# A four-layer sequence kernel: the queries of the third layer are projected between the stages of a scan, and attention is run a group deeper

## What is computed

```python
x = x + attention0(x, cond)          # 16 heads of 16
x = x + scan1(cond, x)               # 128 time steps, four Runge-Kutta stages each: tanh(q) @ coupling.T ...
# layer 2
x1  = ln(x) * (1 + scale1) + shift1                   # scale, shift, gate: from cond, one set per batch
qkv = x1 @ qkv_w + qkv_b                              # 256 -> 3 * 16 * 128
attn = softmax(einsum('bthd,bshd->bhts', q, k) * 128 ** -0.5)
x = x + gate1 * (einsum('bhts,bshd->bthd', attn, v) @ out_w + out_b)
x = x + gate2 * (gelu(x2 @ ffn_w1 + ffn_b1) @ ffn_w2 + ffn_b2)      # x2 = ln(x) * ...
x = x + gru3(cond, x)                # 128 time steps
```

## Time and profile before

| what | value |
|---|---|
| runs (three) | 1753.77, 1754.12 (median), 1755.26 us |
| profiled execution | 1756.03 us, its span 1753.9 us |
| layer 0 | 0 to 260 us |
| scan with its pieces | 260 to 933 us |
| rest of keys and values (finish_kv) | 933 to 1002.6 us |
| attention (attend2) | 1002.6 to 1349.3 us |
| norm, feed-forward, GRU | 1349.3 to 1753.9 us |
| granted TensorE clock, mean | 0.811 of full speed |

### The profile page before, as it was taken

One profiled execution on the slowest core, in us unless ns is written; L12 is line 12 of the kernel. 1 busy time (PEld: TensorE's weight loads), 2 busy tenths in 40 slices (PEclk: granted clock), 3 DMA queues, 4 the chain that ended last, 5 costly groups with the idle time before them and its releaser, 6 DMA issues. The chain is left out here.

```text
span 1753.9 us, 47524 instructions
## 1 busy us (share of the span) xinstructions
PE 1388.7 (79%) x16650; PEld 1077.1 (61%) x16650; DVE 1277.5 (73%) x7020; ACT 807.9 (46%) x3106; POOL 298.3 (17%) x568
## 2 busy tenths in 40 slices
PE   6889874445589549955985799999998489999865
PEld 4377653334466446644664688888885377777764
DVE  4357769999899989998995366666665546676654
ACT  4547843332545255525542255555553644444322
POOL 1015521111011101111111122222120301111110
PEclk8969995555589559955996999999999799999755
DMA  3000000100022002200231573546431300000000
GB/s 128 0 1 2 2 13 38 50 2 2 2 74 110 14 2 92 104 2 2 107 118 79 192 169 97 127 107 141 103 91 48 84 2 3 3 12 6 15 15 14
DMA packets 75014, 95.12 MB, mean 54 GB/s; under 512 B 5692, under 2 KB 46232, under 8 KB 73880
## 3 DMA queue, kind: packets, MB, share of 16 engines
q1 hardware_dynamic: 74336, 89.95, 17.2%
q0 software_dynamic: 272, 2.10, 0.6%
q10 hardware_dynamic: 168, 0.04, 0.0%
HBM read 54.32 MB, written 37.75 MB: 52 GB/s over the span
## 5 line engine op out<-in xcount | busy, mean ns | idle before, releaser
L933 PE MATMUL bank<-s_tanh_hi,coup_hi 128*128 128x16 f16 x2048 | 138.4, 177 | 212.7 <-ACT s_tanh_hi L923 212.4
L933 PEld LDWEIGHTS bank<-s_tanh_hi,coup_hi 128*128 128x128 f16 x2048 | 93.6, 104 | 296.8 <-ACT s_tanh_hi L923 291.1
L1408 ACT ACTIVATE prob<-bank,neg_max 128x128 f32<-128x128 f32 x256 | 90.4, 365 | 129.1 <-DVE neg_max L1457 129.1
L923 ACT ACTIVATE s_tanh_hi<-s_s 128x32 f16<-128x32 f32 x256 | 58.6, 229 | 183.5 <-DVE s_s L778 180.8
L861 POOL TENSOR_SCALAR s_p_scaled<-s_p 128x32 f32<-128x32 f32 x128 | 37.4, 293 | 602.5 <-DVE s_p L844 581.4
L933 PE MATMUL bank<-s_tanh_lo,coup_hi 128*128 128x16 f16 x2048 | 137.3, 177 | 1.8 <-DVE s_tanh_lo L772 0.2
L933 PE MATMUL bank<-s_tanh_hi,coup_lo 128*128 128x16 f16 x2048 | 128.2, 172 | 0.0
L933 PEld LDWEIGHTS bank<-s_tanh_lo,coup_hi 128*128 128x128 f16 x2048 | 90.8, 103 | 32.0 <-DVE s_tanh_lo L772 0.5
L1510 POOL TENSOR_TENSOR prob<-prob,inv 128x512 f32<-128x512 f32 x64 | 66.6, 1040 | 254.4 <-DVE inv L1476 254.4
L1724 PE MATMUL bank<-h_hi,w_h_hi 128*128 128x16 f16 x1536 | 91.2, 172 | 21.8 <-DVE h_hi L1942 21.8
L567 ACT ACTIVATE prob<-bank,neg_max 128x128 f32<-128x128 f32 x256 | 89.9, 377 | 35.6 <-DVE neg_max L515 35.6
(11 more groups left out here) (309 smaller groups left out, 4645.3 us busy)
## 6 DMA issues: line engine op xcount, KB each, us to landing
keys<-tile_stage SPq DMA_DIRECT2D x64, 256.0 KB, 2.0
values<-tile_stage SPq DMA_DIRECT2D x64, 256.0 KB, 2.4
k<-keys SPq DMA_DIRECT2D x64, 256.0 KB, 4.2
v<-values SPq DMA_DIRECT2D x64, 256.0 KB, 6.0
x<-in_L_cond_qkv_w_dram SPq DMA_DIRECT2D x2, 2048.0 KB, 7.3
x_tok<-in_x_dram SPq DMA_DIRECT2D x4, 512.0 KB, 5.5
w_stage<-in_L_cond_qkv_w_dram SPq DMA_DIRECT2D x4, 512.0 KB, 8.1
ow_stage<-in_L_cond_out_w_dram SPq DMA_DIRECT2D x4, 512.0 KB, 5.2
```

The costliest lines, as they stand in the source:

```text
L923: A.activation(th_hi[:, :], s, ACT.Tanh, scale=scale).then_inc(hi_ready, 1)
L933: ins = nc.tensor.matmul(coupled[:, B * m:B * m + B], w[:, o:o + P], th[:, B * c:B * c + B], start=(first and c == 0 and m == 0), stop=(la ...
L1408: last = A.activation(prob[:, grp % 2, h, :], bank[2 + grp % 2][:, T * h:T * h + T], ACT.Exp, bias=neg_max[:, grp % 2, h:h + 1], accum_out ...
```

## The change

Tiles become 48 to a block (`TILES`): of every 12, four are queries, four keys, four values. A plan (`plan`) places pieces by stage; the scan takes 135 tiles (48, 48 and 39), the rest of the kernel 57 (9 left over and the 48 of block 3). The high and low parts of x have one buffer in place of four, so block n's high part waits for the tiles of block n-1. The weights of queries too are split in the scan (96 pieces in place of 64), loaded in six 1 MB parts. In the scan, c = 1 is modulated on POOL (four instructions at each of four time steps), c = 0 on ScalarE (two in a stage). Centring starts at r = 10, tiles at r = 48. Keys and queries are stored so that a unit reads each as one 1 MB transfer of 8 KB rows; a tile is then stored in rows of 512 bytes. The value bias is left out of the values and goes through the output weights into the output bias (32 small products at the end of finish_kv). Attention has no projection, no value bias and no query weights; units are loaded three deep; POOL puts the queries in order of time (`turn`), one head after each group's product with the reciprocal; scores have three banks, outputs two, probabilities four buffers; an output projection of 12 matmuls is spread over two slots.

```diff
-KV_EARLY = 3
-RING = 5
-W_AT, SCALED_AT, LOW_AT, TILES_AT = (20, 72), 24, 36, 45
+EARLY = 3
+RING = 6
+TILES = 3 * H2
+W_AT = 20
...
+def plan():
+    pe, act, dve = {}, {}, {}
+    ready = lambda n: 4 * TB * (n + 1)
+    for n in range(EARLY):
+        r = ready(n)
+        for k in range(4):
+            pe[r + 2 + 2 * k] = ("mean", n, k)
+            pe[r + 20 + k] = ("var", n, k)
+            for c in range(C):
+                dve[r + 2 * k + c] = ("sum", n, k, c)
+                dve[r + 10 + 4 * c + k] = ("centre", n, k, c)
+                dve[r + 27 + 2 * k + c] = ("scaled", n, k, c)
+                dve[r + 39 + 4 * c + k] = ("low", n, k, c)
...
+        i = ready(n) + 48
+        for half in range(2 * TILES):
+            while i in pe:
+                i += 1
+            if i >= 4 * T - 1 or (half % 2 == 0 and i >= 4 * T - 2):
+                break
+            pe[i] = ("tile", n, half // 2, half % 2)
...
+                (37, ("high", n, 0)), (40, ("high", n, 1))]:
...
@@ scan1, gpsimd, behind p_scaled and g3 of step j
+                n, k = divmod(j - TB - 7, TB)
+                if n >= 0 and k < 4:
+                    pool.wait_ge(xhat_ready, 8 * n + C * k + 2)
+                    for b in range(4 * k, 4 * k + 4):
+                        last = G.tensor_scalar(xc[:, 1, TB * b:TB * b + TB], xc[:, 1, TB * b:TB * b + TB],
+                                               g.ada[:, C + 1, b:b + 1], g.ada[:, 1, b:b + 1], MUL, ADD)
+                    last.then_inc(modp_ready, 1)
@@ scan1, scalar
+            def x_high(n, c):
+                if c == 0:
+                    act.wait_ge(mod_ready, 8 * n + 8)
+                    if n:
+                        act.wait_ge(tile_full, TILES * n)
+                else:
+                    act.wait_ge(modp_ready, 4 * n + 4)
+                A.activation(g.x_hi[:, c, :], xc[:, c, :], ACT.Copy).then_inc(xh_ready, 1)
@@ finish_kv, tensor: 3 left-over tiles before the variance, 6 behind it, then block 3
+            for v in range(min(3, LEFT)):
+                tile(v)
...
+            for v in range(3, LEFT):
+                tile(v)
             pe.wait_ge(xl_ready, 2 * C)
+            for v in range(LEFT, len(todo)):
+                tile(v)
+            pe.wait_ge(g.d_ow, 16)
+            for c in range(C):
+                for h in range(H2):
+                    last = M.matmul(bank[0][:, c:c + 1], g.ow_raw[:, h, P * c:P * c + P], g.vec[:, V_VB + h:V_VB + h + 1],
+                                    start=(h == 0), stop=(h == H2 - 1))
@@ attend2, tensor
+            def scores(v):
+                u, b = divmod(v, 4)
+                pe.wait_ge(q_turned, 4 * u + 4)
+                pe.wait_ge(d_k[u % AHEAD], 16 * (u // AHEAD + 1))
+                if v >= 3:
+                    pe.wait_ge(p_ready, v - 2)
...
+            for i in range(SLOTS + 1):
+                if in_range(i):
+                    scores(i)
+                if in_range(i - 2):
+                    transposed(i - 2)
+                if in_range(i - 3):
+                    valued(i - 3)
+                u, part = divmod(i - 7, 4)
+                if 0 <= u < UNITS:
+                    projected(u, part // 2, part % 2)
@@ attend2, vector, slot i: maximum of i, probT of i-2, o_l of i-3, reciprocal of i, and with part odd the four additions
@@ attend2, scalar, slot i: four exponentials of i, o_h of i-3
@@ attend2, gpsimd
+            def turn(u, h):
+                pool.wait_ge(d_q[u % AHEAD], 16 * (u // AHEAD + 1))
+                if u >= 2:
+                    pool.wait_ge(s_full, 4 * (u - 1))
+                G.tensor_copy(q2[:, u % 2, h, :, :].rearrange("p b (n t) -> p n b t", n=4), q_raw[:, u % AHEAD, h, :, :, :]).then_inc(q_turned, 1)
+            for h in range(HG):
+                turn(0, h)
...
+            for i in range(GROUPS):
+                pool.wait_ge(inv_ready, i + 1)
+                G.tensor_tensor(prob[:, i % PR, :, :], prob[:, i % PR, :, :],
+                                inv[:, i % PR, :].unsqueeze(2).broadcast_to([P, HG, T]), MUL).then_inc(pn_ready, 1)
+                if i < GROUPS - 4:
+                    turn(i // 4 + 1, i % 4)
```

More of the change, by code:

```diff
@@ L999, in finish_kv @@
     late = slice(TB * n, T)
-    TILES = 2 * H2
+    todo = [(u // TILES, u % TILES) for u in range(g.tiles_out, TILES * (EARLY + 1))]
+    LEFT = TILES * EARLY - g.tiles_out
     def modulate(eng, c, sem_done):
@@ L1070, in _ @@
                                     SUB).then_inc(xc_ready, 1)
+            for v in range(1, min(3, LEFT), 2):
+                evacuate(dve, v, copy)
             chunk0 = modulate(dve, 0, mod_ready[0])
@@ L1078, in _ @@
                 next(chunk0)
+            for v in range(3, LEFT, 2):
+                evacuate(dve, v, copy)
             for h in range(2):
@@ L1097, in _, with copy @@
             A = nc.scalar
+            def copy(out, src, i):
+                if i % 12 < 8:
+                    return A.activation(out, src, ACT.Identity, bias=tile_bias(g, i),
+                                        scale=D2 ** -0.5 if i % 12 < 4 else 1.0)
+                return A.activation(out, src, ACT.Copy)
             for h in range(2):
@@ L1271, in attend2 @@
     bank = g.bank
-    STEPS = 4
-    def slots():
-        for p in range(UNITS + 2):
-            for k in range(4):
-                yield p, k, 4 * (p - 1) + k
+    SB, TBK, OB, YB = bank[0:3], bank[4:6], (bank[3], bank[6]), bank[7]
+    SLOTS = GROUPS + 6
+    in_range = lambda v: 0 <= v < GROUPS
     with nc.Block() as block:
@@ new lines, in transposed, with valued @@
+            def transposed(v):
+                pe.wait_ge(pn_ready, v + 1)
+                if v >= 2:
+                    pe.wait_ge(t_out, v - 1)
+                for h in range(HG):
+                    last = M.transpose(TBK[v % 2][:, T * h:T * h + T], prob[:, v % PR, h, :], g.ident[:, :])
+                last.then_inc(t_full, 1)
+            def valued(v):
+                u, b = divmod(v, 4)
+                pe.wait_ge(d_v[u % AHEAD], 64 * (u // AHEAD + 1))
+                pe.wait_ge(t_out, v + 1)
+                if v >= 2:
+                    pe.wait_ge(ol_ready, v - 1)
+                for h in range(HG):
+                    last = M.matmul(OB[v % 2][:, T * h:T * h + T], v2[:, u % AHEAD, b, D2 * h:D2 * h + D2],
+                                    probT[:, v % 2, T * h:T * h + T], start=True, stop=True)
+                last.then_inc(o_full, 1)
@@ L1363, in _ @@
                         pe.wait_ge(y_out, 2 * u + m)
-                    ms = slice(P * m, P * m + P)
-                    three(bank[7][:, :], [(ow_h[:, h, ms], ow_l[:, h, ms], o_h[:, u % 2, h, :],
-                                           o_l[:, u % 2, h, :]) for h in range(HG)], y_full)
-        def conversions(p, k):
-            if p % 4 == 3 and p < UNITS - 1 and k == 3:
-                yield "w", p // 4 + 1
-            if p % 4 == 2 and 6 <= p < UNITS and k == 0:
-                yield "ow", p // 4
-        first = [("w", 0), ("ow", 0)]
+                ms = slice(P * m, P * m + P)
+                for h in (2 * half, 2 * half + 1):
+                    for w, (sh, mv) in enumerate(((ow_h, o_h), (ow_h, o_l), (ow_l, o_h))):
+                        last = M.matmul(YB[:, :], sh[:, h, ms], mv[:, u % 2, h, :], start=(h == 0 and w == 0),
+                                        stop=(h == HG - 1 and w == 2))
+                if half:
+                    last.then_inc(y_full, 1)
+            for i in range(SLOTS + 1):
[8 more added lines that the diff above has]
+                    projected(u, part // 2, part % 2)
         @block.scalar
```

590 lines of the change are left out of this document (255 added, 335 removed).

## The result

The changed kernel takes 1777.04 us (median of four runs, 1776.31 to 1780.15) against 1753.99: 1.0134 times the time before, 95% interval 1.0122 to 1.0146. It is slower, as forecast, but by 23 us where 10 were forecast. The profiled execution took 1777.18 us, its span 1775.5, 21.6 longer than before.

A forecast was written before the change was run, and what follows sets the result against it. Attention was taken as bound by a VectorE-ScalarE loop, by TensorE only in two slots of four; the change adds a once-a-unit wait. Scan -0.5, finish_kv +26.5, attention -16: +10.0 us, forecast 1764, range 1750 to 1782.

The forecast's parts named there:

- The slot arithmetic: Attention: slots of 3.48 us without additions, 4.52 with them, and one long slot a unit of 5.79 plus the turn, 0.75.
- the opening: Start of attention: the maximum of group 4 some 27.5 us in, against 28.6 before; -1, between -5 and +4.
- First tile of block 3: finish_kv: nine tiles of earlier blocks in the norm chain put this tile 4.5 us later, some 24 us in.
- Rival 1: Attention: the fourth turn is never the last thing the scores wait for; a unit takes 16.0, total 1718 us; chance 0.12.
- Rival 2: Stores of finish_kv and the scan's tail at the DMA limit, turn at its upper end: about 1775; with Rival 3, 0.20.
- The row cost of 0.0059: DMA share per GB/s for 512-byte rows, against 0.0027 for 2 KB rows: share 0.92 at 190 GB/s in finish_kv.
- Rival 3: Scan: POOL and VectorE hinder each other, +4 not +1.5 at r = 40, three times: 1772; with Rival 2, 0.20.
- The long slot, step "scores 1.06": Attention, once a unit: scores waiting for the fourth turn take 1.06 us, within a slot of 5.79 plus the turn.
- The small products, "5 taken, +2.2 net": End of finish_kv: 32 bias products take between 3.4 and 6.4 us, 5 taken; partly hidden by last evacuation and store, +2.2.
- "I take the clock to stay up: -3.0": finish_kv: after about three us idle the run of tiles stays at full clock, saving 3.0 us, at worst 0.
- The scan: Weight pieces +2.6, half tiles -1.7, centring -3.2, modulation -3.7, r = 40 +4.5, end +1.2; sum given as -0.5 us.
- the wait at r = 40: Scan: ScalarE's high part of c = 1 waits for POOL's last modulations; +1.5 us three times, +4.5.

The follow-up runs named there:

- Experiment 1: Changed kernel with POOL's turn put ahead of its product with the reciprocal in each attention slot: 1718.15 us, 0.9785 of the kernel before.
- experiment 5: Changed kernel with the output bias summed on POOL in finish_kv, leaving 2 one-column products in place of 32: 1769.65 us, 1.007 of the kernel before.
- experiment 3: Changed kernel with 12 extra TensorE products, results overwritten, ahead of each scores that wait for the fourth turn: 1764.12 us, 1.0042 of the kernel before.
- experiment 11: Changed kernel with only POOL's clears of earlier stages' semaphores moved behind its last product: 1780.89 us, 1.0148 of the kernel before.
- experiment 4: Changed kernel with the output bias products and their add moved from the end of finish_kv to the start of attention: 1779.81 us, 1.0137 of the kernel before.
- experiment 6: Changed kernel with POOL's base added in eight 128x512 pieces behind the turns of slots 0 to 7: 1774.39 us, 1.0102 of the kernel before.
- experiment 9: Changed kernel with turn ahead, bias summed on POOL, base in pieces and later split, plus semaphore clears behind POOL's last product: 1710.61 us, 0.9748 of the kernel before.

## Why the prediction was off

**Right.** The direction, and its reason: two slots of four in attention were not bound by TensorE's work, and what the other two gave back (5.2 us and more before, 4.4 after) went in good part into the long slot; in finish_kv the tiles cost their full 1.36. The slot arithmetic held to 0.1 us for all three kinds at full clock, the opening too (group 4 is 27.2 us into the stage, forecast 27.5). First tile of block 3: 24.3 us into finish_kv, worked out 23.65. Rival 1 fell (49.8 us of waits for the turn). Experiment 1 gives the 1718 that it named, but to the microsecond by luck: 59 us below 1777, not 46 below 1764. Rival 2 fell: share 0.57 at 189 GB/s is 0.0030 a GB/s, beside 0.0027 with 2 KB rows, and the turn takes 0.61 and not 1.04. The row cost of 0.0059 that the prediction drew from attention's loads doesn't hold for stores. Loads were not measured apart: attention's whole window went from 0.0041 a GB/s to 0.0036 when its loads in 512-byte rows were gone. The Trainium skill's figure ("DMA: Bandwidth & Descriptors", Specifications: 512 bytes suffice for the full rate) agrees with this trace as far as it goes, up to 189 GB/s. Rival 3 fell for this kernel: the stage at r = 40 takes 2.48, under the 2.74 of the forecast, and POOL's 48 modulations in the scan take 0.40 us in the median and 0.52 at most. Its mechanism does exist, as experiment 5 shows with larger instructions.

**Wrong, by size.**
- *The long slot, step "scores 1.06".* The duration came from a slot in which TensorE had just been busy, and was put into one where it had idled for 3.4 us. What failed is this term: the scores, and the transposes and values' product behind them, run at 0.50, the scores taking 1.74. That is +11.7 in 13 units (experiment 3: 10.6 of it come back), against 4.2 gained there because the turn takes 0.61 and not 0.75, the other slots 3.44 and 4.44 and the splits 1.67. The rest of what attention missed is +0.6 in groups 4 to 8 (their long slot took 7.34) and +1.5 behind group 60. Of that, 0.8 is the slot behind the last long one, 5.26 where experiment 3 has 4.46, and 0.7 stays unexplained.
- *The small products, "5 taken, +2.2 net".* They took 9.51 and added 6.2 (9.8 behind the last tile against 3.6). Even the upper bound of 6.4 for their length was too low: the windows show 36 records in the 4 us from 1022 on and 20 in the next 4, in which the clock is 0.96 and then 0.50 (below). At the full clock they would be some 7, an estimate from 64 x 0.11. The evacuation and store did hide 3.6, as said.
- *"I take the clock to stay up: -3.0".* In this trace the first tile again ran at the low level (0.80 for its first matmul) after only 2.46 us idle. The run of 48 tiles lasted 67.1 us against 46.5 for 32, +20.6 where 18.8 was forecast. But in eight of the twelve other traces it lasted 65.6, +19.1: there the term held, and the other 1.5 come and go with the execution.
- *The scan.* -2.9 and not -0.5: centring (r 10 to 17) and modulation (r 28 to 35) gained what was forecast, 10.6 us for eight stages each, the wait at r = 40 cost 1.2 a time and not 1.5, and the end 0.8 instead of 1.2. The prediction's own terms add up to -0.3, not -0.5. Some 1.3 us are in none of them.

```profile
1022.00:1026.00 4.00, 4.00 (x36) 4.00 (x36) 0.00 (x0) 0.00 (x0) 0.00 (x0) 0.96 0.21 82
1026.00:1030.00 4.00, 4.00 (x20) 4.00 (x21) 0.00 (x0) 0.00 (x0) 0.00 (x0) 0.50 0.00 0
```

**Open.** Executions of one kernel differ by up to 8 us (experiment 11). Where traces differ without an edit, it is in layer 0 (258.0 to 262.1 us to the first tanh), in stages of the scan behind a pause of TensorE, where a low clock lasts for a few stages more or fewer, and in the first tile of block 3 (25.8 to 27.3 us after the last tanh, 27.4 to 29.1 where POOL sums the bias). What decides that was not tried.

## What to carry to other kernels

When work moves off an engine, price what the engine will do in the gap: here TensorE, idle for 3.4 us, soon ran at half speed, and the first products behind the gap must be taken from rows at that level. In a queue worked in order, put the instruction whose input is long there ahead of the one that waits for the end of the loop; here that order alone decided between 23 us lost and 38 gained. And when the last thing in a wait is removed, name the next one before counting the gain: under the adds lay the clears, under the clears a load.

## What the runs showed of the hardware

- Adding work made the kernel faster: 180 products more, 13 us less, with a mean clock of 0.99 in the loop in place of 0.91 (experiment 3).
- The clock fell while TensorE was shown busy without a break: in the two windows above it does nothing but one-column products with full weight loads. One record takes 0.11 us at 0.96 and 0.20 at 0.50; all 64 at the low level 13.79 us (experiment 4).
- Clearing semaphores holds POOL's queue for some 7.7 us, which shows nowhere as busy time, only as a wait of 7.77 us that is put down to the reciprocal (experiment 6); with the clears elsewhere the first product comes 2.60 us behind the first maximum and not 5.46 (experiment 9).
- POOL's reordering copy of 128x512 takes 0.61 us, its product of two inputs of that size 1.04.
- VectorE and POOL slowed each other down where both had large operands: four subtractions of 128x256 took 1.67 to 2.12 us beside POOL's sums and 1.43 without them (experiment 5). POOL's small modulations of 128x32 in the scan kept near their 0.40 us (0.52 at most).
